# Attention stage of a transformer layer: the causal mask added by TensorE, the block loop software-pipelined

## The reference

```
xn = _layernorm(x)
q = (xn @ Wq + bq).reshape(b, h, t, dh)
k = (xn @ Wk + bk).reshape(b, t, h, dh).transpose(0, 2, 3, 1)
v = (xn @ Wv + bv).reshape(b, t, h, dh).transpose(0, 2, 1, 3)
logits = einsum('bhtd,bhds->bhts', q, k) * scale
mask = triu(full((t, t), -inf), k=1)
weights = softmax(logits + mask)
out = einsum('bhts,bhsd->bhtd', weights, v) ... @ Wo + bo
# feed-forward: ternary-quantised weights (groups of 64), silu(gate) * up,
# rms norm, projection with ternary-quantised weights
x = x + attention(xn) + ffn(xn)
```

## Time and profile before

| | us |
|---|---|
| median of 2 runs | 7861.03 (7822.4 to 7899.66) |
| profiled execution | 7824.59 |
| its span, slowest core (7) | 7823.0 |
| spans of the 8 cores | 7774.5 to 7823.0 |
| attention on core 7: first logits to the last product into Obig | 999.6 to 2394.5 |
| output projection, first and last matmul | 2454.9 to 2566.9 |
| feed-forward | from about 2600 to the end |

### The profile page before, as it was taken

The page is one execution under the profiler, slowest core; times in us unless marked ns, Lnnn a source line. Parts: engine busy times, 40 slices in busy tenths (PEclk is TensorE's granted clock), DMA queues, the critical chain, the costliest instruction groups (busy, mean ns, idle before and its releaser), DMA issues.

```text
span 7823.0 us, 32993 instructions; the slowest of 8 cores (7774.5 to 7823.0 us)
## 1 busy us (share of the span) xinstructions
PE 3194.5 (41%) x10968; PEld 1121.8 (14%) x10968; DVE 2755.2 (35%) x2263; ACT 439.9 (6%) x480; POOL 146.2 (2%) x268
## 2 busy tenths in 40 slices
PE   0476945555555322222222222200005655555556
PEld 0133411111112100000000000000002222222222
DVE  5211112112211455555555555579990000000000
ACT  2000012222220000000000000000000000000000
POOL 0000000000000000000000000000000000000000
PEclk9988966666657656566566565555559976676799
DMA  5433110000003433333333333357875543223355
GB/s 157 80 64 69 38 35 11 11 11 16 11 5 70 91 79 79 75 79 80 77 79 81 81 81 81 80 105 137 137 134 188 194 99 63 61 62 62 72 191 177
DMA packets 996877, 646.13 MB, mean 83 GB/s; under 512 B 894179, under 2 KB 902500, under 8 KB 989540
## 3 DMA queue, kind: packets, MB, share of 16 engines
q10 hardware_dynamic: 752384, 314.63, 16.7%
q0 software_dynamic: 38016, 142.62, 11.4%
q1 hardware_dynamic: 206310, 186.77, 8.2%
HBM read 463.57 MB, written 134.22 MB: 76 GB/s over the span
## 4 chain that ended last, share of the span: by engine, by line
PE 37%; DVE 33%; DMA 18%; ACT 5%; issue 4%; ACTq 2%; DVEq 1%; POOL 0%; SPq 0%; POOLq 0%
PE PS L700 8%; PE PS L705 8%; DMA wpT<-wptdram 6%; DVE quot L588 6%; DVE m2b L595 6%; DVE wnat L598 6%; DVE gsum L577 6%; DMA wT<-wnat 4%; DMA wT<-wgqdram 4%; ACT Pt L480 4%; PE PS L817 3%; PE PS L492 3%; PE PS L496 3%; PE PS L389 3%; PE PS L345 3%
## 5 line engine op out<-in xcount | busy, mean ns | idle before, releaser
L700 PE MATMUL PS<-XT_own,wT 128*128 128x512 bf16 x2048 | 964.6, 471 | 2122.5 <-DMA wT<-wnat 1795.8
L705 PE MATMUL PS<-XT_own,wT 128*128 128x512 bf16 x2048 | 955.8, 467 | 0.0
L817 PE MATMUL PS<-wpT,Hbig 128*128 128x512 bf16 x2048 | 500.0, 389 | 1032.3 <-DMA wpT<-wptdram 998.2
L720 DVE TENSOR_TENSOR Hbig<-silu_sb,PS 128x512 bf16<-128x512 bf16 x128 | 88.0, 687 | 2030.9 <-ACT silu_sb L716 2030.9
L700 PEld LDWEIGHTS PS<-XT_own,wT 128*128 128x128 bf16 x2048 | 238.5, 116 | 2518.5 <-issue 2391.5
L492 PE MATMUL PS<-Pt,onc 128*1 128x512 bf16 x512 | 259.4, 507 | 530.6 <-ACT Pt L480 530.6
L595 DVE SCALAR_TENSOR_TENSOR m2b<-quot,m2b 128x2048 bf16<-128x2048 bf16 x192 | 440.1, 2292 | 20.7 <-DVE m2b L593 0.9
L598 DVE TENSOR_TENSOR wnat<-m2b,gsum 128x2048 bf16<-128x2048 bf16 x192 | 440.1, 2292 | 20.6 <-DVE m2b L595 0.9
L588 DVE TENSOR_TENSOR quot<-wnat,grc 128x2048 bf16<-128x2048 bf16 x192 | 440.2, 2292 | 20.4 <-DVE grc L586 0.5
L577 DVE TENSOR_REDUCE gsum<-wnat 128x32 f32<-128x2048 bf16 x192 | 438.3, 2283 | 25.0 <-DMA wnat<-wgu 11.6
L817 PEld LDWEIGHTS PS<-wpT,Hbig 128*128 128x128 bf16 x2048 | 187.2, 99 | 1344.8 <-issue 1171.1
(11 more groups left out here) (67 smaller groups left out, 1993.9 us busy)
## 6 DMA issues: line engine op xcount, KB each, us to landing
wpT<-wptdram ACTq DMA_DIRECT2D x256, 512.0 KB, 3.4
wnat<-wgu POOLq DMA_DIRECT2D x128, 512.0 KB, 5.2
wgqdram<-wnat SPq DMA_DIRECT2D x128, 512.0 KB, 3.5
wnat<-wp POOLq DMA_DIRECT2D x64, 512.0 KB, 8.8
wptdram<-wpt SPq DMA_DIRECT2D x64, 512.0 KB, 5.3
Xf<-x_kv SPq DMA_DIRECT2D x16, 1024.0 KB, 6.1
Xf<-x_q SPq DMA_DIRECT2D x8, 1024.0 KB, 6.3
Wsb<-Wq POOLq DMA_DIRECT2D x16, 512.0 KB, 6.7
```

The source lines that it names most:

```text
L700: e.matmul(PS[:, (gb + rh) * 512:(gb + rh) * 512 + w], wT[par * 2][:, k * 128:(k + 1) * 128], XT_own[:, k * TQ + scol0 + rh * 512: k * TQ ...
L705: ii = e.matmul(PS[:, (2 + rh) * 512:(2 + rh) * 512 + w], wT[par * 2 + 1][:, k * 128:(k + 1) * 128], XT_own[:, k * TQ + scol0 + rh * 512: ...
L817: ii = e.matmul(PS[:, sc * 2048 + dt * 512: sc * 2048 + (dt + 1) * 512], Hbig[:, k * SHALF + row * 128: k * SHALF + row * 128 + 128], wpT[ ...
```

## The change

Three things change inside the head loop, and a small constant is added.

1. The mask is no longer added by VectorE. For the blocks with ps = 0 each logits matmul is preceded by a matmul with a bf16 identity (ident_b) as weights and the mask columns as the moving operand, which starts the sum in PSUM; the matmul with Kh adds to it.
2. The emission is rotated by one block: the logits and the exponential of block g are emitted before the sum and output matmuls of block g-1. The last block's sum and output matmuls come alone at the end of the head. The buffers are the same two and two.
3. The sum and output matmuls of a block are grouped: ones, ones, Vh, Vh.
4. ident_b is a new input of 32 KB, loaded in the "dc" chain after ident; it takes 256 bytes of each partition, and all tiles allocated behind it move up by that. The logits matmuls now also wait for ident_b and for the mask's load (before, the mask addition waited for it).

```diff
+    ident_b = at("ident_b", [128, 128], BF16)
...
+    t_idb = P.dma("sync", "dc", lambda e: e.dma_start(out=ident_b[:, :], in_=idb_d))
...
-        for ps in range(2):
-            for jc in range(NCH):
...
-                tl = P.op("pe", mml,
-                          deps=[kh_load[h], l_free[lpar], qbig_done])
-                if ps == 0:
-                    def msk(e, jc=jc, lpar=lpar):
-                        return e.tensor_tensor(
-                            PS[:, lpar * 1024: lpar * 1024 + TQ],
-                            PS[:, lpar * 1024: lpar * 1024 + TQ],
-                            mask_sb[:, jc * TQ:(jc + 1) * TQ], AL.add)
-                    tm = P.op("dve", msk, deps=[tl, mload])
...
+        def emit_logits(gsb):
...
+                for rh in range(2):
+                    if ps == 0:
+                        e.matmul(
...
+                            ident_b[:, :],
+                            mask_sb[:, jc * TQ + rh * 8 * RR:
+                                    jc * TQ + (rh + 1) * 8 * RR],
+                            start=True, stop=False)
+                    ii = e.matmul(
...
+                        Kh[h % 2][:, gsb * 128:(gsb + 1) * 128],
+                        qv[:, rh * 8:(rh + 1) * 8, h * RR:(h + 1) * RR],
+                        start=(ps != 0), stop=True)
+                return ii
+            return P.op("pe", mml,
+                        deps=[kh_load[h], l_free[lpar], qbig_done, t_idb,
+                              mload])
...
+                for rh in range(NHF):
+                    e.matmul(PS[0:1, 3072 + rh * 512:3072 + rh * 512 + WQ],
+                             onc[:, :],
+                             Pt[ppar][:, rh * 512:rh * 512 + WQ],
+                             start=st, stop=sp)
+                for rh in range(NHF):
+                    ii = e.matmul(
+                        PS[:, 2048 + rh * 512:2048 + rh * 512 + WQ],
+                        Vh[h % 2][:, gsb * 128:(gsb + 1) * 128],
...
+        tl0 = emit_logits(0)
+        texp_q[0] = emit_exp(0, tl0)
+        l_free[0] = texp_q[0]
+        for gsb in range(1, 2 * NCH):
+            lpar = gsb % 2
+            tl = emit_logits(gsb)
+            texp_q[gsb] = emit_exp(gsb, tl)
+            l_free[lpar] = texp_q[gsb]
+            tav = emit_av(gsb - 1, texp_q[gsb - 1])
+            pt_free[(gsb - 1) % 2] = tav
+            d_last = tav
+        tav = emit_av(2 * NCH - 1, texp_q[2 * NCH - 1])
```

More of the change, by code:

```diff
@@ L94, in build_nc @@
                            kind="ExternalInput").ap()
+    idb_d = nc.dram_tensor("ident_b", [128, 128], BF16,
+                           kind="ExternalInput").ap()
     onr_d = nc.dram_tensor("ones_row", [1, 128], F32,
@@ L450, in build_nc, with mml @@
         last_exp = None
-        for ps in range(2):
-            for jc in range(NCH):
[L453 to L459, removed]
+        def emit_logits(gsb):
+            ps = gsb // NCH
+            jc = gsb % NCH
+            lpar = gsb % 2
+            def mml(e, h=h, gsb=gsb, jc=jc, ps=ps, lpar=lpar):
+                qv = Qbig[:, :].rearrange("p (c q) -> p c q", c=DB)
+                ii = None
+                for rh in range(2):
+                    if ps == 0:
+                        e.matmul(
@@ L460, in mml @@
                             PS[:, lpar * 1024 + rh * 8 * RR:
                                lpar * 1024 + (rh + 1) * 8 * RR],
[L462 to L465, removed]
-                tl = P.op("pe", mml,
-                          deps=[kh_load[h], l_free[lpar], qbig_done])
-                if ps == 0:
-                    def msk(e, jc=jc, lpar=lpar):
-                        return e.tensor_tensor(
-                            PS[:, lpar * 1024: lpar * 1024 + TQ],
-                            PS[:, lpar * 1024: lpar * 1024 + TQ],
-                            mask_sb[:, jc * TQ:(jc + 1) * TQ], AL.add)
-                    tm = P.op("dve", msk, deps=[tl, mload])
-                else:
-                    tm = tl
@@ L477, in build_nc @@
[L477 to L506, removed]
+                            ident_b[:, :],
[3 more added lines that the diff above has]
+                    ii = e.matmul(
+                        PS[:, lpar * 1024 + rh * 8 * RR:
+                           lpar * 1024 + (rh + 1) * 8 * RR],
+                        Kh[h % 2][:, gsb * 128:(gsb + 1) * 128],
+                        qv[:, rh * 8:(rh + 1) * 8, h * RR:(h + 1) * RR],
+                        start=(ps != 0), stop=True)
@@ new lines, in mml, with emit_exp, exp_ @@
+                return ii
+            return P.op("pe", mml,
+                        deps=[kh_load[h], l_free[lpar], qbig_done, t_idb,
+                              mload])
+        def emit_exp(gsb, tl):
+            ps = gsb // NCH
+            lpar = gsb % 2
+            ppar = gsb % 2
+            def exp_(e, ps=ps, lpar=lpar, ppar=ppar):
+                b = sh1[:, 0:1] if ps == 0 else p2b[:, 0:1]
+                return e.activation(Pt[ppar][:, :],
+                                    PS[:, lpar * 1024: lpar * 1024 + TQ],
+                                    AF.Exp, bias=b, scale=SCL)
+            return P.op("act", exp_, deps=[tl, pt_free[ppar], t_p2, t_sh1])
@@ new lines, in emit_av, with mmav @@
+        def emit_av(gsb, texp):
+            ppar = gsb % 2
+            def mmav(e, h=h, gsb=gsb, ppar=ppar):
+                st = (gsb == 0)
+                sp = (gsb == 2 * NCH - 1)
+                ii = None
+                for rh in range(NHF):
[7 more added lines that the diff above has]
+                        Vh[h % 2][:, gsb * 128:(gsb + 1) * 128],
+                        Pt[ppar][:, rh * 512:rh * 512 + WQ],
+                        start=st, stop=sp)
+                return ii
+            return P.op("pe", mmav,
+                        deps=[texp, vh_load[h], t_onc] +
+                        ([av_free, rs_free] if gsb == 0 else []))
@@ new lines, in build_nc @@
+        texp_q = {}
+        tl0 = emit_logits(0)
+        texp_q[0] = emit_exp(0, tl0)
+        l_free[0] = texp_q[0]
+        for gsb in range(1, 2 * NCH):
+            lpar = gsb % 2
+            tl = emit_logits(gsb)
[5 more added lines that the diff above has]
+        tav = emit_av(2 * NCH - 1, texp_q[2 * NCH - 1])
+        pt_free[(2 * NCH - 1) % 2] = tav
@@ L507, in build_nc @@
+        d_last = tav
+        last_exp = texp_q[2 * NCH - 1]
         kh_free[hp] = d_last
@@ L950, in host_prep @@
             "mask1": mask1, "pass2b": p2b, "ident": ident,
+            "ident_b": ident.astype(BF),
             "ones_col": ones_col, "ones_row": ones_row,
```

## The result

The changed kernel takes 7129.95 us (median of 11 runs, 7084.26 to 7200.98), the kernel before 7888.5 us (median of 10, 7822.4 to 7914.07). The ratio is 0.905, with a 95% interval of 0.9005 to 0.9094. The forecast was 7112 us in a range of 7060 to 7225.

What follows compares the result with a forecast made beforehand. No engine bounds the whole; in attention TensorE, ScalarE and VectorE take turns in a serial ring. 7824.6 less 722 (16 heads at 45.1 us) plus 2 gives 7104.6, forecast as 7112 us, range 7060 to 7225.

Steps and rivals of the forecast that it cites:

- The ring is cut, TensorE bounds the stage: Attention blocks: TensorE works during the exponential; masked blocks 1.90 us, unmasked 1.47, heads 41.9 us against 87.0.
- the exponential's path: Attention block, last logits matmul's start to first sum matmul: 1.73 us at full clock, just covered by 1.78 of TensorE work.
- Spacings: Attention matmuls at full clock: 0.215 us between like ones, about 0.09 more per change between 128x1 and 128x128 weights.
- the lower bound taken: Two ones matmuls in a row in a block: 0.215 us apart taken, 0.31 the other bound, costing 23 us.
- The clock: Attention heads: each begins at 1.2 GHz, then dense TensorE work gets the full clock, as in the K projection.
- Coming up: Start of each head: rising from the low clock costs 2.1 us once per head, bounds 0 and whole head low.
- The head's end: Last Vh matmul to next head's logits: 11.8 us unchanged, of reciprocal 6.55, spread matmuls 3.75, copy 1.0 and hand-overs.
- The extra load: New ident_b load in the "dc" chain, which the bias rows wait for: +2 us, bounds 0 and 2.1.
- The sum: Whole kernel: 7824.6 less 722 us of attention plus 2 for the load makes 7104.6 us against the profiled execution.
- Rival 3: Attention: overlap does not come, only mask and grouping count, 114 us gained, 7713 us, within 2%; chance 0.03.
- Rival 1: Attention: the clock stays low, spacings 0.43 us, heads 63.0 us, 7443 us in all; chance 0.07.
- Rival 2: Attention: eight dense cores get 0.81 of the clock, 5.5 us more a head, 7194 us in all; chance 0.05.

Runs made afterwards that it cites:

- mask_rot: The changed kernel with sum and output matmuls alternating again (ones, Vh, ones, Vh) instead of grouped; 7185.69 us, heads 44.5 us.
- mask_group: The changed kernel without the rotation: mask by TensorE, matmuls grouped, each block's four behind its own logits; 7508.8 us, ratio 0.9548.
- before_fill: The kernel before with 10 (masked) or 5 (other blocks) unused matmuls behind each block's logits, while TensorE waited; 7688.09 us, ratio 0.9801.
- after_keep: The changed kernel with 26 unused matmuls in TensorE's wait for the reciprocal at each head's end; 7125.36 us, ratio 0.9078.
- the late division: Changed kernel with square ones tile; VectorE first copies output and sums to SBUF, reciprocal and product follow during the next head; 6921.07 us, ratio 0.8759.
- mask_only: The kernel before with only the mask moved to TensorE, block order not rotated, matmuls alternating; 7622.38 us, ratio 0.9679.
- early_logits: The changed kernel with the next head's first two logits groups and exponentials moved ahead of the spread matmuls; 7150.14 us, ratio 0.904.
- rot_only: The kernel before with only the rotation: mask addition on VectorE, sum and output matmuls alternating; 7265.94 us, ratio 0.9209.
- square_ones: The changed kernel with a 128x128 tile of ones replacing the 128x1 column, spread matmuls and copy left out; 7022.6 us, ratio 0.8908.

## Why the prediction was right

Point by point, by its own steps:

- **The ring is cut, TensorE bounds the stage.** Right. Blocks 1.90 and 1.47 us were forecast, 1.92 and 1.50 measured; the exponential's path of 1.73 us against 1.78 us of work is just covered, as the wait of 5.0 us in the whole stage shows.
- **Spacings.** 0.215 us between like matmuls and 0.09 for a change of weight width: right, and mask_rot measures the 0.09 by itself. Two ones matmuls in a row are 0.21 apart (a pair takes 0.59, one 0.38), the lower bound taken.
- **The clock.** The dense blocks get 2.4 GHz, and each head begins low, as in the K projection. Coming up costs less than the 2.1 us taken, by one head of core 7:

```profile
1422.01 0.59 PE L464 MATMUL PS<-mask_sb,ident_b 128*128 128x512 bf16 x1 [1.26 <-ACT rc_sb L547]
...
1425.44 0.59 PE L500 MATMUL PS<-Pt,onc 128*1 128x512 bf16 x2 [0.18 <-issue]
```

  Eight matmuls take 3.43 us there, where 8 x 0.215 + 0.09 = 1.81 are due: 1.6 more, 0.18 of it idle. The blocks cost 8 x (1.92 + 1.49) = 27.3 us instead of 27.0. The head came out at 41.7 us for 41.9; that it is so close is in part luck, errors of some tenths of a us with opposite signs.
- **The head's end**, 11.8 us, is unchanged: spread matmuls 3.75 us behind a wait of 6.80.
- **The extra load.** TensorE's first matmul starts at 15.78 us in the profile after, against 14.41 in the earlier trace rows: 1.4 us for the 2 forecast.
- **The sum.** 7104.6 us was the forecast against the profiled execution; the profiled one took 7093.11. Attention gave 724.5 us (999.6 to 2394.5 before, 1004.2 to 1674.6 on core 3 after) of the 722 forecast, and began 4.6 us later, not 2. The 11 us left over lie behind attention, on a stretch of 5428 us on core 7 before and 5417 on core 3 after. They lie within what the cores differ by: on core 7 that stretch went from 5429 to 5409 us, on core 3 from 5411 to 5417. So nothing shows that the stages behind attention changed.

What was off is in a rival, not in the forecast. Rival 3 priced the mask and the grouping, without the overlap, at 7713 us, within 2%. mask_group is that kernel, and its ratio of 0.9548 is clearly faster. The step that failed is its price of a masked block, 1.39 and 0.18 less and "0.86 for two matmuls at 0.43" more: it held the clock of the stage fixed while changing what TensorE does in it. The measured head is 22.0 us shorter than before where that step gives 7.1 (8 x 0.89), and the clock went from 0.62 to 0.87. before_fill shows that the clock alone can be worth 12.1 us a head, near the 14.9 that the step misses.

Rival 1 (low clock in attention) did not come. Rival 2 (a clock between the two levels) did not come for attention as a whole, but it exists. It was priced for attention alone; where it shows, core 3 of after_keep, it costs more ahead of attention (106 us) than in it (heads of 40.6 us against 40.1 on core 5). See the last section.

## What to carry to other kernels

Read a serial ring on two engines twice: once for its period, and once for the clock that the idle time in it costs TensorE; a part that shortens the ring can be worth several times its own length (the mask move saves 8 x 0.53 = 4.2 us of ring by the prices at the low clock, and was worth 18.0), and the same part little once the ring is cut (3.3). Before rotating a loop, set the work that will lie beside the wait against the path from the last producer to the first consumer: here 1.78 us against 1.73 was enough. When the blocks are dense, look at what is between them: the square tile of ones and the late division together were worth 209 us, more than the mask move and the grouping on top of the rotation (136 us). By the heads the tile gave 7.5 us each and the late division 7.0, the mask move and the grouping 6.1.

## What the runs showed of the hardware

- Short waits, one in every block, are enough to hold the clock low. In the kernel before no wait for the exponential exceeded 3.2 us, the masked blocks got 0.50 to 0.57 in all fifteen heads, and the stage got 0.62. Unused matmuls in these waits brought 0.91 and a faster kernel.
- A third level of the clock, on pairs of neighbouring cores. In the profile of after_keep, in the K projection (500 to 680 us), core 3 and its neighbour core 2 are granted 0.83 and the cores 0, 1 and 4 to 7 are granted 1.00 with the same program. The 0.83 is a mean: from 540 to 630 us core 3 has 0.81 in every 10 us, with its matmuls 0.262 us apart. Here core 3, then core 5:

```profile
500.00:680.00 180.00, 180.00 (x701) 75.29 (x700) 32.30 (x43) 0.00 (x0) 0.00 (x0) 0.83 0.09 32
```

```profile
500.00:680.00 180.00, 180.00 (x836) 81.61 (x835) 39.17 (x53) 0.00 (x0) 0.00 (x0) 1.00 0.11 39
```

In the same stretch cores 4 and 5 have 0.82 in mask_only, cores 2 and 3 have 0.86 in early_logits, cores 0 and 1 have 0.91 in before_fill, and in rot_only two pairs fall at once (2 and 3 with 0.91, 4 and 5 with 0.83); none does in the profiles of before and after. In after_keep core 3 ends its first head about 106 us later than core 5 (first reciprocal at 1143.2 against 1037.1 us). In each of these five profiles the slowest core is one of such a pair. The Trainium skill ("TensorE: Matmul & The Clock Gate", Part 1) states 13/16 of the clock, 0.81, from the third core of a die with dense matmuls on, for the whole die. The level agrees. The extent does not: all eight cores are dense there, most keep 1.00, and the cores that fall are one pair or two. That this makes the spread of the times (7084 to 7201 us for the changed kernel) is likely and not shown, since only one execution of each kernel has a profile. The spans of the cores fit it: at 7200.98 us cores 2 and 3 took 7160.7 and 7199.4, and no other core over 7133.7.
- VectorE's reciprocal takes 6.55 us for 1024 elements on one partition (L535) and 6.56 on 128 (square_ones).
